# Attention heads as row tiles of TensorE, with both score stages issued together in one fused cross-attention and expert kernel

## The chip, the cores and the metric

The kernel runs on one core of a Trainium2 chip. The metric is the device time of one execution, in microseconds. Inside it five engines work in parallel, each on its own queue in program order and tied to the others by semaphores: PE (TensorE), DVE (VectorE), ACT (ScalarE), POOL (GpSimd) and SP (SyncE, which here only issues DMAs). "PEld" is the loading of PE's stationary operand.

## What is computed

32 sequences of 128 tokens and 128 channels (`x`) attend to 32 contexts of 77 tokens and 96 channels (`ctx`), with 16 heads of 8 channels. A mixture of 8 experts with two chosen per token follows. Cut to what matters:

```
x1  = x + tanh(g_xattn) * attention(layernorm(x), ctx)
        q, k, v = LN(layernorm(x)) @ Wq + bq, LN(ctx) @ Wk + bk, LN(ctx) @ Wv + bv
        w = softmax(q @ k.T / sqrt(8)), one head at a time;  y = w @ v
out = x1 + tanh(g_ffn) * experts(layernorm(x1))
        logits = z @ w_router;  two best experts, softmax over their two logits
        y_e = square(relu(z @ w1[e])) @ w2[e];  out = sum of the two y_e by their gates
```

## The kernel before

The 32 sequences are 8 tiles of 4 batches. One *step* `i` has four *slots* `j` (`slots`, L253), and in a slot each engine works on several batches at once, in an order written out by hand in its `step` function. `near[k]` is the batch `k` places ahead of batch `(i, j)`, so in slot `(i, j)` the first score stage of `near[3]` and `near[2]`, the second of `near[1]` and `near[0]`, the values of `near[-1]` and the routing of `near[-2]` are made, beside two experts (`e[1]`, `e[2]`) of an earlier tile. Steps run from -2 to 9: two steps fill the pipeline, steps 8 and 9 drain it (`closing`, L616). A tile therefore passes every fourth slot.

The attention of a batch has two score stages. The first (`scores`, L496) gives `q @ k.T` with the tokens on partitions, so that DVE can take each head's maximum (`maximum`, L1032, the TENSOR_REDUCE of L1038). Its negative is split into two parts, turned by PE (`max_turn`, L506), copied out by ACT (`max_store`, L745) and written by SP's DMA into rows of the queries' tile (`max_rows`, L341). The second stage (`scoresT`, L513) computes the scores again with the keys on partitions and with those rows added, so that ACT's `exponent` (L815) gives `exp(score - max)` directly. PE multiplies that by the values (`values`, L528), ACT takes the heads out (`evacuate_heads`, L803), PE turns them (`turn_heads`, L552), and DVE scales, adds and takes the statistics (`attended`, L1052: reciprocal, scale, add, stats, aggregate). POOL makes the root (`rstd`, L1381), DVE normalises (`normalise2`, L1082), PE turns the result (`turn`, L559) and routes it (`route`, L564), and DVE picks the two best (`routed`, L1095).

Queries and keys are float32 split into a high and a low part, and the product is taken as three terms (high by high, high by low, low by high), stacked along the contraction: 8 channels of 4 heads by 3 terms is 96 rows. `ks` holds the keys block by block with zeros between heads, so one matmul of 96 rows and 312 columns gives a group of 4 heads in the first stage (4 matmuls a batch), and the second stage takes 16 matmuls of 104 rows and 128 columns a batch. Per tile SP fills these tiles by 8 DMAs of `k_hi` (L324) and 3 of the queries (L338), and POOL by 4 of `k_lo` (L1416).

An expert unit is `hidden` (L577, three matmuls of 512 columns), DVE's `gated` (L1151, relu times the gate, line L1157), ACT's `square` (L821, line L824) and PE's `output` (L589, line L592, eight matmuls). `finish` (L1179) adds a tile's result.

The small PSUM tenants share two banks `ab_0` and `ab_1` in the fixed turn of `AB_USES` (L33). Each use takes the other bank, so a use waits in `claim` (L417) until the use two places before it has been taken out. `keep_on` (L455) issues matmuls without a use for their result.

## Time and profile before

| | us |
|---|---|
| median of 3 runs | 323.77 |
| lowest and highest of them | 321.93, 325.83 |
| the profiled execution, its own time | 321.95 |
| its span (first to last instruction) | 320.2 |
| PE, DVE, ACT, POOL busy in the span | 293.1, 232.8, 178.8, 104.9 |

The profile is of one execution. Busy times are unions over an engine's instructions: PE counts as busy from a matmul's start to its modelled end, so neighbouring matmuls overlap in it. An instruction's "mean ns of one" is its whole length; the distance between the starts of two neighbours is shorter where they are pipelined. The granted clock (PEclk) is a share of 2.4 GHz. A chain piece "DVE u L1157 0.57" is the part of that instruction that lies on the chain of waits.

### The profile page before, as it was taken

Reading aid. Unit: us, or ns where it says so; the run is one execution under the profiler, and the core shown is the slowest. Engines: PE = TensorE matmul, PEld = TensorE weight load, DVE = VectorE, ACT = ScalarE, POOL = GpSimd, SP = SyncE. Lnnn points to the kernel's source line nnn. Section 1 sums busy time; section 2 is a strip of 40 time slices with the busy share of each in tenths; the row PEclk is TensorE's granted clock in tenths of the full one; section 3 lists DMA queues with packets and bytes.
Section 4 is the critical chain, followed back from the end, with each engine's and each line's share of the span. In section 5 each row is a group of like instructions: output and inputs, shape, how many; then the busy total and the mean of one; then the engine's idle time right before and its main releaser. Section 6 shows DMA issues by size and latency. Waiting matters only on the chain.

```text
span 320.2 us, 7854 instructions
## 1 busy us (share of the span) xinstructions
PE 293.1 (92%) x2837; PEld 242.5 (76%) x2837; DVE 232.8 (73%) x934; ACT 178.8 (56%) x412; POOL 104.9 (33%) x193
## 2 busy tenths in 40 slices
PE   7986988799999999998999899999999889989995
PEld 5555576587788788887888787888888778778784
DVE  7886487666869886887688768886767666645765
ACT  1522656544666566654765566566656545565473
POOL 6594415254204712471246224422412210220010
PEclk9997879967999999999999999999999999999998
DMA  3353201087255927593639463917382530070011
GB/s 71 95 152 87 53 12 53 8 138 101 81 191 110 133 75 232 94 126 98 231 67 132 101 196 97 137 26 210 122 130 39 192 125 22 4 269 29 2 35 33
DMA packets 18919, 32.92 MB, mean 103 GB/s; under 512 B 4922, under 2 KB 12059, under 8 KB 18881
## 3 DMA queue, kind: packets, MB, share of 16 engines
q1 hardware_dynamic: 12176, 23.39, 31.1%
q0 software_dynamic: 3216, 7.66, 11.0%
q10 hardware_dynamic: 3488, 1.38, 1.7%
q8 instruction: 22, 0.36, 0.5%
q14 instruction: 17, 0.13, 0.2%
HBM read 21.04 MB, written 2.21 MB: 73 GB/s over the span
## 4 chain that ended last, share of the span: by engine, by line
PE 43%; DMA 21%; DVE 12%; SPq 11%; issue 5%; ACT 4%; ACTq 2%; POOL 1%; DVEq 0%; POOLq 0%
DMA qs<-q_lo 14%; SPq L324 9%; PE y L592 8%; PE c L547 6%; PE ab L503 5%; PE s L524 4%; DMA gb<-gates_scratch 4%; DVE negm L1038 2%; DVE u L1157 2%; PE h L458 2%; SPq L338 2%; PE h L585 2%; PE ab L570 2%; PE h L587 2%; DMA gates_scratch<-gatesT 2%
## 5 line engine op out<-in xcount | busy, mean ns | idle before, releaser
L1038 DVE TENSOR_REDUCE negm<-ab 128x4 f32<-128x308 f32 x128 | 60.6, 476 | 41.4 <-PE ab L503 40.1
L819 ACT ACTIVATE p<-s 77x512 f32<-77x512 f32 x128 | 74.5, 583 | 18.6 <-PE s L524 18.4
L524 PEld LDWEIGHTS s<-qs,ks 104*77 104x77 f32 x512 | 56.8, 155 | 12.6 <-issue 4.6
L524 PE MATMUL s<-qs,ks 104*77 104x128 f32 x512 | 62.2, 246 | 0.8 <-ACT p L819 0.8
L592 PE MATMUL y<-w2s,hs 128*128 128x128 f32 x448 | 60.4, 279 | 1.4 <-ACT hs L824 1.2
L503 PE MATMUL ab<-ks,qs 96*128 96x312 f32 x128 | 50.9, 399 | 8.6 <-DMA qs<-q_lo 4.2
L592 PEld LDWEIGHTS y<-w2s,hs 128*128 128x128 f32 x448 | 55.1, 193 | 3.4 <-ACT hs L824 2.5
L1385 POOL TENSOR_SCALAR rs<-mv 128x1 f32<-128x1 f32 x32 | 7.3, 228 | 144.7 <-DVE mv L1079 144.7
L824 ACT ACTIVATE hs<-u 128x512 f32<-128x512 f32 x56 | 34.9, 623 | 14.5 <-DVE u L1157 14.4
L1157 DVE SCALAR_TENSOR_TENSOR u<-h,gb 128x512 f32<-128x512 f32 x56 | 38.0, 678 | 4.0 <-DMA gb<-gates_scratch 2.5
L503 PEld LDWEIGHTS ab<-ks,qs 96*128 96x128 f32 x128 | 25.3, 198 | 13.5 <-issue 6.2
L547 PE MATMUL c<-p,vs 77*32 77x128 f32 x1024 | 35.4, 280 | 0.0
L585 PE MATMUL h<-x_hi,w_lo 128*128 128x512 f32 x64 | 31.3, 490 | 0.4 <-DVE top L1101 0.4
L805 ACT ACTIVATE oT<-c 128x256 f32<-128x256 f32 x32 | 12.3, 384 | 34.7 <-PE c L547 34.7
L547 PEld LDWEIGHTS c<-p,vs 77*32 77x32 f32 x1024 | 26.6, 111 | 5.1 <-issue 4.8
L587 PE MATMUL h<-x_hi,w_hi 128*128 128x512 f32 x64 | 25.2, 394 | 0.0
L586 PE MATMUL h<-x_lo,w_hi 128*128 128x512 f32 x64 | 25.2, 394 | 0.0
L1416 POOL DMA_DIRECT2D ks<-k_lo x32 | 18.3, 577 | 17.9 <-issue 10.8
L749 ACT ACTIVATE mT<-ab 32x128 fp32r<-32x128 f32 x32 | 8.4, 264 | 24.2 <-PE ab L509 24.1
L1387 POOL TENSOR_TENSOR rs<-rs,neg_half 128x1 f32<-128x1 f32 x32 | 18.3, 572 | 2.7
L1378 POOL TENSOR_TENSOR nrm<-nrm,neg_half 77x4 f32<-77x4 f32 (+1 forms) x16 | 17.3, 1082 | 1.3
L1085 DVE TENSOR_SCALAR xn<-x,mv,rs 128x128 f32<-128x128 f32 x32 | 11.4, 355 | 7.3 <-POOL rs L1387 6.8
(129 smaller groups left out, 503.4 us busy)
## 6 DMA issues: line engine op xcount, KB each, us to landing
gb<-gates_scratch SPq DMA_DIRECT2D x14, 768.0 KB, 5.8
gb<-gates_scratch SPq DMA_DIRECT2D x7, 512.0 KB, 3.9
qs<-q_hi SPq DMA_DIRECT2D x12, 256.0 KB, 6.5
ks<-k_hi SPq DMA_DIRECT2D x60, 39.0 KB
x_res<-in_x_dram POOLq DMA_DIRECT2D x8, 256.0 KB, 5.2
out_dram<-y_out POOLq DMA_DIRECT2D x7, 256.0 KB, 6.3
x_sb<-in_x_dram POOLq DMA_DIRECT2D x6, 256.0 KB, 5.0
qs<-q_lo SPq DMA_DIRECT2D x6, 256.0 KB, 8.7
```

The source lines that it names most:

```text
L324: sp.dma_start(ks[r:r + HD, par, :, i, :].bitcast(F32), k_hi[QROWS * i:QROWS * i + QROWS].rearrange("p b n -> p (b n)").bitcast(F32))\
L503: nc.tensor.matmul(p[:, 0:J * NP].rearrange("t (i n) -> t i n", n=NP), qs[0:QR, par, c, T * j:T * j + T], ks[0:QR, par, c, :, NP * j:NP * ...
L524: mm = nc.tensor.matmul(p[0:N, T * i:T * i + T], ks[:, par, c, i, NP * j:NP * j + N], qs[:, par, c, T * j:T * j + T], start=True, stop=True)
L547: mm = nc.tensor.matmul(bank_c[VT * i:VT * i + VT, r:r + T], vs[:, par, j, NC * i + c, :], p32[:, m % LR, T * i:T * i + T], start=(c == 0) ...
L585: nc.tensor.matmul(p[:, :], w1_lo[:, e, :], x_hi[:, par, :], start=True, stop=False)
L586: nc.tensor.matmul(p[:, :], w1_hi[:, e, :], x_lo[:, par, :], start=False, stop=False)
L587: nc.tensor.matmul(p[:, :], w1_hi[:, e, :], x_hi[:, par, :], start=False, stop=True).then_inc(h_ready, 1)
L592: mm = nc.tensor.matmul(bank_y[:, D * b:D * b + D], hs[:, e % 2, T * b:T * b + T], w2s[:, e, :], start=(e == 0 and b == 0), stop=(e == E - ...
L819: nc.scalar.activation(p32[:, m % LR, :], src, ACT.Exp).then_inc(p_done, 1)
L824: nc.scalar.activation(hs[:, e % 2, :], u[:, e % 2, :], ACT.Square).then_inc(hs_done, 1)
L1038: nc.vector.tensor_reduce(negm[:, :, c], bank_ab[bank][:, 0:J * NP].rearrange("t (i n) -> t i n", n=NP)[:, :, 0:N], AX.X, ALU.max, negate= ...
L1157: nc.vector.scalar_tensor_tensor(out=u[:, e % 2, :], in0=bank_h[e % 2][:, :], scalar=0.0, in1=gb[:, par, e, :], op0=ALU.max, op1=ALU.mult) ...
```

## The change

The heads become row tiles. A head group `i` owns rows `32i` to `32i+31` of `qs` and `ks`: 24 rows of three terms and 2 rows of the maximum. The zeros between heads go. Each head is one matmul of 24 rows and 78 columns in the first stage and one of 26 rows and 128 columns in the second. `both_scores` issues four of them in turn on four different row groups: two of the first stage for one batch, two of the second for another; a call has 16 matmuls and a slot has two calls. The first call (heads of groups `c`, `d` and the second pair of exponents) stands after `turn_heads`; the second (`a`, `b` and the first pair) ends the slot. The values of a batch come first in a slot (behind `turn`) and wait for all its exponents. Keys are projected one slot earlier (slot 2). The three query DMAs of 256 KB become 12 of 64 KB, 4 on SP and 8 on POOL; a maximum takes two DMAs instead of one. The first tile's queries are put in place by matmuls with a selector; tile 1 takes the DMA path. `p32` has 6 buffers instead of 5. The orders of ACT and DVE are rewritten, and the 104-row memsets of `ks` go. In the diff, cut to its core, the lines that the new orders replace are left out; they stand in the kernel above.

```diff
+    (-1, "turn2"), (0, "s1c2"), (0, "s1d2"), (-1, "route2"), (0, "mT2"), (0, "s1a3"), (0, "s1b3"),
+    (-1, "turn3"), (-1, "route3"), (0, "s1c3"), (0, "s1d3"), (0, "mT3"), (1, "v"), (1, "s1a0"), (1, "s1b0"),
+    (0, "turn0"), (1, "s1c0"), (1, "s1d0"), (0, "route0"), (2, "ctxT"), (1, "mT0"), (2, "k"), (2, "xT"),
+    (1, "s1a1"), (1, "s1b1"),
+    (0, "turn1"), (1, "s1c1"), (1, "s1d1"), (0, "route1"), (2, "q"), (1, "mT1"), (1, "s1a2"), (1, "s1b2"),
 ]
...
+        qs = sb("qs", [J * ROWS, 2, NC, GT], F32R)
+        ks = sb("ks", [J * ROWS, 2, NC, G * NP], F32R)
...
+        def stack_keys(eng, s, par, term, i, landing):
+
+            r = ROWS * i + HD * term
+            src = k_lo if term == 1 else k_hi
+            eng.dma_start(ks[r:r + HD, par].rearrange("p c n -> p (c n)").bitcast(F32),
+                          src[ROWS * i:ROWS * i + ROWS].rearrange("p b n -> p (b n)").bitcast(F32))\
+                .then_inc(landing[par], 16)
+
+        def stack_queries(eng, s, par, term, i, landing):
+
+            r = ROWS * i + HD * term
+            src = q_lo if term == 2 else q_hi
+            eng.dma_start(qs[r:r + HD, par].rearrange("p c t -> p (c t)").bitcast(F32),
+                          src[ROWS * i:ROWS * i + ROWS].bitcast(F32)).then_inc(landing[par], 16)
...
+            def stack_q(s, par, term):
+
+                sp.wait_ge(hi_q, s + 1)
+                for i in range(J):
+                    stack_queries(sp, s, par, term, i, q_stacked)
 
             def max_rows(s, par, j):
                 bank, n = ab(s, f"mT{j}")
                 sp.wait_ge(ab_taken[bank], n)
-                sp.dma_start(qs[QR:MR, par, :, T * j:T * j + T].bitcast(F32),
-                             mT[:, j % 2, :].bitcast(F32)).then_inc(m_in[j], 16)
+                for a in range(SPLITS):
+                    sp.dma_start(qs[KEYED + a::ROWS, par, :, T * j:T * j + T].bitcast(F32),
+                                 mT[H * a:H * a + H, j % 2, :].bitcast(F32)).then_inc(m_in[j], 16)
 
             def spread_gates(s, par):
...
+            def both_scores(first, first_pair, second, second_pair):
+
+
+                if first:
+                    s, par, j = first
+                    if j == 0 and first_pair == 0:
+                        stacked(s, par)
+                    banks = [claim(s, f"s1{'abcd'[i]}{j}") for i in (2 * first_pair, 2 * first_pair + 1)]
+                if second:
+                    t, tp, b = second
+                    if t < 2 and (b, second_pair) == (0, 0):
+                        pe.wait_ge(ones_in[tp], 16 * SPLITS)
+                    if second_pair == 0:
+                        pe.wait_ge(m_in[b], SPLITS * (16 * t + 16))
+                    m = NC * (G * t + b) + 2 * second_pair
+                    if m > 0:
+                        pe.wait_ge(p_done, m)
+                for c in range(NC):
+                    if first and (s, j, first_pair) == (0, 0, 0):
+                        pe.wait_ge((q_kept_act, q_kept_dve)[c % 2], c // 2 + 1)
+                    for k in range(2):
+                        if first:
+                            r, (p, ready) = ROWS * (2 * first_pair + k), banks[k]
+                            mm = nc.tensor.matmul(p[:, NP * c:NP * c + NP], qs[r:r + KEYED, par, c, T * j:T * j + T],
+                                                  ks[r:r + KEYED, par, c, NP * j:NP * j + NP], start=True, stop=True)
+                            if c == NC - 1:
+                                mm.then_inc(ready, 1)
+                        if second:
+                            r = ROWS * FIRST_EXPS[2 * second_pair + k]
+                            mm = nc.tensor.matmul(bank_s2[k][0:N, T * c:T * c + T],
+                                                  ks[r:r + SHIFTED, tp, c, NP * b:NP * b + N],
+                                                  qs[r:r + SHIFTED, tp, c, T * b:T * b + T], start=True, stop=True)
+                            if c == NC - 1:
+                                mm.then_inc(s2_ready, 1)
...
+                    pe.wait_ge(p_done, NC * n + NC)
                 r = T * (c // 2)
                 for i in range(J):
                     mm = nc.tensor.matmul(bank_c[VT * i:VT * i + VT, r:r + T], vs[:, par, j, NC * i + c, :],
-                                          p32[:, m % LR, T * i:T * i + T], start=(c == 0), stop=(c % 2 == 1),
+                                          p32[:, (NC * n + FIRST_EXPS.index(i)) % LR, T * c:T * c + T], start=(c == 0), stop=(c % 2 == 1),
                                           skip_group_check=True)
                 mm.then_inc(pv_done, 1)
...
             def turn(s, par, j):
                 pe.wait_ge(post_d, at(POST, G * s + j, "normed"))
-                p, ready = claim(s, f"turn{j}", j in (0, 3) and not last(s))
+                p, ready = claim(s, f"turn{j}")
                 nc.tensor.transpose(p[:, 0:T], xn2[:, :], ident[:, :]).then_inc(ready, 1)
 
             def route(s, par, j):
                 if (s, j) == (0, 0):
                     pe.wait_ge(experts_in, 16 * 3)
-                if last(s):
-                    pe.wait_ge(xT_done, G * s + j + 1)
+                pe.wait_ge(xT_done, G * s + j + 1)
...
                     if near[-1] and not values_first:
                         for c in range(NC):
                             values(*near[-1], c)
+                    if held:
+                        output(*held)
+                    if j == 1 and near[-2]:
                         route(*near[-2])
+                    warm(i, j, 0)
                     if near[-1]:
                         turn_heads(*near[-1])
+                    both_scores(near[2], 1, near[0], 1)
+                    if (i, j) == (0, 0):
+                        project_keys(1)
                     if e[1] is not None:
                         hidden(sf, pf, e[1])
+                    if j != 1 and near[-2]:
+                        route(*near[-2])
+                    if turned and i != -1:
                         transpose_ctx(turned[0])
                     if turned and turned[0] == 0:
                         keep_on(bank_s2[1], 1)
                         project_keys(0)
+                        transpose_x(0)
                     if (i, j) == (-2, 3):
+                        first_queries()
                         keep_on(bank_s2[1], 2)
+                        select_queries()
+                    elif made:
+                        project_queries(made[0])
                     if e[2] is not None:
                         hidden(sf, pf, e[2])
+                    warm(i, j, 1)
+                    if near[2]:
+                        max_turn(*near[2])
+                    if keyed and j == 2:
+                        project_keys(keyed[0])
+                        transpose_x(keyed[0])
+                    if turned and i == -1:
+                        transpose_ctx(turned[0])
+                    if j == 1 and spread(i - 1):
                         gates_turn(i - 1)
+                    if j == 1 and nxt:
+                        project_values(nxt[0])
+                    if e[1] is not None and (i, j) != (S - 1, 2):
                         output(sf, pf, e[1])
+                    warm(i, j, 2)
+                    both_scores(near[3], 0, near[1], 0)
+                    if turned and i == -1:
                         transpose_x(turned[0])
...
                     if j == 1 and exists(i - 1):
                         gate_exp(i - 1)
+                    if near[0]:
                         exponent(*near[0], 2)
+                        exponent(*near[0], 3)
+                    if (i, j) == (0, 0):
+                        evacuate_k(*keyed)
+                    if turned and i != -1:
                         evacuate_ctxT(turned[0])
                     if turned and turned[0] == 0:
                         evacuate_k(*turned)
+                        evacuate_xT(0)
+                    if (i, j) == (-2, 3):
+                        first_queries()
+                        keep_queries()
+                    elif made:
+                        evacuate_q(*made)
+                    if e[1] is not None:
                         squared(sf, e[1])
+                    if near[2]:
+                        max_store(*near[2])
+                    if keyed and j == 2:
+                        evacuate_k(*keyed)
+                        evacuate_xT(keyed[0])
+                    if turned and i == -1:
+                        evacuate_ctxT(turned[0])
+                    if j == 1 and nxt:
+                        evacuate_v(*nxt)
                     if (i, j) in PREPARING:
                         prepare_experts(PREPARING.index((i, j)))
                     if e[2] is not None:
                         squared(sf, e[2])
+                    if near[1]:
+                        exponent(*near[1], 0)
+                        exponent(*near[1], 1)
+                    if turned and i == -1:
                         evacuate_xT(turned[0])
+                    if j == 1 and spread(i - 1):
+                        gate_rows(i - 1)
                     if near[-1]:
                         evacuate_turned(*near[-1])
...
+                    take(ahead, 2)
+                    if near[-2]:
+                        low_x(*near[-2])
+                    if j == 1 and near[-2]:
                         routed(*near[-2])
+                    take(gating)
+                    take(post, 4)
                     take(top_scores)
                     take(post)
+                    take(gating)
+                    take(top_scores, 3)
+                    take(gating, 2)
+                    if i == 0:
+                        take(ahead, 2)
+                    if (i, j) == (0, 0):
+                        take(prepare, 2)
+                    if j == 2 and exists(i - 2):
+                        finish(i - 2, par)
+                    if j != 1 and near[-2]:
+                        routed(*near[-2])
+                    if e[1] is not None:
                         gated(sf, pf, e[1])
+                    take(gating, 3)
+                    if near[-1]:
                         normalise2(*near[-1])
+                    if e[2] is not None:
+                        gated(sf, pf, e[2])
                     take(prepare, 9)
+                    if near[3]:
+                        take(tops_of(near[3]), 2)
...
+            def stack_rest_q(s, par):
+                pool.wait_ge(hi_q, s + 1)
+                apart(pool)
+                for i in range(J):
+                    stack_queries(pool, s, par, 1, i, q_rest_stacked)
+                bank, n = ab(s, "q")
+                pool.wait_ge(ab_taken[bank], n)
+                apart(pool)
+                for i in range(J):
+                    stack_queries(pool, s, par, 2, i, q_rest_stacked)
```

## Rows read from the trace of the kernel before

**Rows 1.** The page, part 1: busy time of PE

```profile
PE 293.1 (92%) x2837; PEld 242.5 (76%) x2837; DVE 232.8 (73%) x934; ACT 178.8 (56%) x412; POOL 104.9 (33%) x193
```

**Rows 2.** The page, part 4: chain that ended last, by engine

```profile
PE 43%; DMA 21%; DVE 12%; SPq 11%; issue 5%; ACT 4%; ACTq 2%; POOL 1%; DVEq 0%; POOLq 0%
```

**Rows 3.** Stretches: length, engines' busy us, granted clock, DMA share, GB/s

```profile
70.00:80.00 10.00, 9.76 (x80) 7.84 (x78) 5.83 (x33) 5.46 (x16) 5.35 (x8) 0.70 0.81 108
...
127.60:161.20 33.60, 31.53 (x343) 27.17 (x342) 26.48 (x112) 20.50 (x50) 12.24 (x22) 1.00 0.62 131
...
290.00:320.00 30.00, 25.17 (x198) 21.44 (x196) 19.02 (x73) 15.98 (x31) 2.43 (x5) 0.97 0.06 19
```

**Rows 4.** Chain of waits, 127 to 166 us: start, us on the chain, what

```profile
128.84 0.68 SPq L324
...
135.84 9.67 DMA qs<-q_lo
...
151.38 0.28 DVE o L1061
...
152.09 0.29 DVE st L1075
...
153.06 0.57 DVE u L1157
153.64 0.40 DVE negm L1038
154.03 0.14 issue
154.17 0.63 PE ab L436 x4
154.80 0.89 PE y L592 x8
155.69 0.11 PE ab L562
...
156.84 1.01 PE c L547 x32
157.85 0.32 PE ab L570 x2
158.17 0.25 PE ab L503
158.42 0.27 PE s L524 x4
158.69 0.24 PE c L556 x2
158.93 0.53 PE ab L445 x2
159.46 0.23 PE h L585
...
161.22 0.86 PE ab L453 x2
```

**Rows 5.** Groups by line and shape: busy us, mean ns | idle before

```profile
L1038 DVE TENSOR_REDUCE negm<-ab 128x4 f32<-128x308 f32 x128 | 60.6, 476 | 41.4 <-PE ab L503 40.1
...
L1157 DVE SCALAR_TENSOR_TENSOR u<-h,gb 128x512 f32<-128x512 f32 x56 | 38.0, 678 | 4.0 <-DMA gb<-gates_scratch 2.5 <-PE h L587 1.6
L824 ACT ACTIVATE hs<-u 128x512 f32<-128x512 f32 x56 | 34.9, 623 | 14.5 <-DVE u L1157 14.4
...
L1416 POOL DMA_DIRECT2D ks<-k_lo x32 | 18.3, 577 | 17.9 <-issue 10.8 <-PE s L524 7.1
...
L805 ACT ACTIVATE oT<-c 128x256 f32<-128x256 f32 x32 | 12.3, 384 | 34.7 <-PE c L547 34.7
...
L1057 DVE RECIPROCAL rden<-c 128x16 f32<-128x16 f32 x32 | 8.1, 252 | 0.8 <-PE c L556 0.8
...
L1183 DVE TENSOR_TENSOR y_out<-x,y 128x512 f32<-128x512 f32 x7 | 4.7, 678 | 2.1 <-PE y L592 2.1
```

443 lines of the change are left out of this document (121 added, 322 removed).

## The prediction

> **What bounds the kernel now.** I read the page's busy times first [rows 1]: PE is busy 293.1 of 320.2 us, and no other engine passes 73%. The chain of waits by engine [rows 2] gives PE only 43%, with 21% on DMA and 11% on SP's queue, so PE is full for most of the time but something beside it ends last now and then. The stretches [rows 3] say how the middle looks: one tile, 127.6 to 161.2 us, takes 33.6 us with PE busy for 31.5 and DVE for 26.5. The chain in order of time [rows 4] then shows the other thing: SP issues eight key DMAs, 0.68 us each, from 128.84, then the queries', and the last of them (135.84) takes 9.67 us to land. It lands at 145.5, and PE's next first-stage matmul waits for it by 1.5 us. So a tile is about 31.5 us of PE work and 1.5 to 2 us of waits: PE bounds it, because the hand-written order lets DVE and ACT run under it.
>
> **The change, part by part.** *The score matmuls.* Before, a batch costs 4 first-stage matmuls 0.25 us apart and 16 second-stage ones, 0.27 us for four [rows 4]: 1.0 + 1.1 = 2.1 us, 8.3 a tile. After, it has two calls of 16. No row shows row groups side by side. The nearest is the values' group, 32 matmuls of 32 output columns on four column groups in 1.01 us, 32 ns each [rows 4], where a full-width one of the output takes 0.89/8 = 111 ns. From below I take half of that, 0.25 us a call (row groups overlap fully, and half the work of each); from above 16 times the 0.27/4 = 67 ns of today's second stage, 1.1 us, if nothing overlaps. I take the 32 ns of the nearest row, 0.5 us, plus 0.15 for getting in and out: 0.65 a call, 5.2 a tile. PE's own work then falls by 3.1 us a tile to about 28.4 (bounds 25.4 to 32). All else equal, that would be the gain.
>
> The row shows 32 ns a matmul with no gap beside the group of values longer than the 0.15 us of its neighbours. The Trainium skill (TensorEngine Tiling (Array Packing), Tiling Modes) says that a change of tiling mode, not of tile, drains the TensorE. Here each slot gains four such changes; the rule gives no time for one, and with an estimated 0.1 us more for each than I have taken a tile would come out 1.6 us longer.
>
> *The order.* All else is not equal, and I take this to decide. In the new order each slot is one ring of steps in which every engine waits for the one before. Walk through a slot of a middle tile, j = 0, with time 0 at the start of PE's `turn`:
> - PE: turn 0.11, values 1.01, output of the held expert 0.89, heads turned 0.24 [rows 4]: 2.35. With the last one's tail and the hand-over, 2.5.
> - DVE can only now begin `attended`, and all that follows stands behind it in its queue: reciprocal 0.25, scale 0.28, add 0.28, each with 0.04 of hand-over, and stats, whose tail the next instruction covers, 0.2: 1.15 together [rows 4, 5]. Then the reductions of c and d, 0.40 from start to start [rows 4], an aggregate between them (0.1), the end of the last reduction (0.1), the two parts of the maximum (an estimate of 0.4 for two short dependent instructions) and the router's two (0.2): 5.25. Only then `gated(e[1])`, 0.66: 5.9.
> - ACT squares it, 0.62 [rows 5], with two hand-overs: 6.6. PE has been through with its first call, both `hidden` and the maximum's transpose at about 5.2, and waits 1.4 us for this.
> - PE: output(e1) 0.89: 7.5. Only then the second call, which makes heads a and b of the next batch: 0.65, 8.15.
> - DVE reduces a (0.48 and 0.04), 0.14 to PE (the "issue" in [rows 4]): 8.8. `turn`, which opens the next slot, claims the bank of a, since each use takes the bank of the use two places before, and all of PE's queue stands behind it.
>
> So this slot is 8.8 us. The other slots of a tile add to the ring:
> - j = 1: five steps of `gate` (difference and four searches, denominator, conversion, comparisons: an estimate of 1.25) stand ahead of gated(e1), and `gates_turn` and `project_values` ahead of output(e1). Gates are ready 0.6 after gated(e1) at 7.15, with a hand-over 7.9; the values' eight matmuls are of the kind that takes 0.89 in rows 4: 8.8; output 9.7, call 10.35, reduction 11.0.
> - j = 2: `finish` 0.68 [rows 5] ahead of gated(e1), so the square ends at 7.25; ACT then stores the maximum (0.27), whose bank `transpose_x` (0.63 in [rows 4]) needs, and output(e1) is behind that: it starts at 8.0 instead of 6.6, slot 10.2.
> - j = 3: the query projection, 0.86 against the keys' 0.53 [rows 4], comes ahead of hidden(e2), and ACT's copy of it (0.69, an estimate from the 0.62 of the square) ahead of the square: 0.5, slot 9.3.
>
> Sum 8.8 + 11.0 + 10.2 + 9.3 = 39.3 us for a tile that takes 33.4 now (33.6 in rows 3; its neighbours 33.4 and 33.0): +5.9, four such tiles (steps 2 to 5): +24. Step 6 has no keys and queries to make: 8.8 + 11.0 + 9.5 + 8.8 = 38.1 against about 33.3: +5. Step 7: slots 0 and 1 as far as they exist: +4. Step 1 has experts only in its second half, and its first half is freed of one output in the ring: +2.4. Steps -2 to 0 have no expert and no such ring. They lose the memsets and the row-wise query projections, gain the selection, and tile 1 now waits for 24 DMAs that SP and POOL issue at 0.6 to 0.7 us each: I take 0, with 4 us to either side. The drain (steps 8, 9) is not touched. Sum 24 + 5 + 4 + 2.4 = +35.
>
> *The transfers.* Before, q_lo could go only after SP's eight key DMAs, and landed 15.5 us after it was made. Now POOL issues it after four DMAs of keys and four of q_hi, 12 times 0.58 us [rows 5] = 7 us in all, and SP issues 8 + 4 at 0.68 = 8.2 us after the maximum's two. In slots of 9 us both have more than 18 us from the projection to the need. Hidden; if slots were 7 us, as PE's work alone would allow, 24 DMAs in 14 us would be as late as now. The second DMA of each maximum, 0.68 us on SP, has a slot to land in. POOL's queue puts `rstd` of the next slot 0 behind q_lo's DMAs: by my walk they are all issued some 3.5 us into that slot, and the statistics come at 4.3. Hidden by 0.8; without that cover up to 2 us a tile.
>
> The profiled execution is 321.95 us (span 320.2 and 1.75 around it); the median shown is 323.77, the lowest 321.93. 321.95 + 35 = 357.
>
> **Rivals.** *A: PE stays the bound and the saving is real.* The ring would have to be shorter than PE's 28.4 us a tile, which asks for slots of 7.1 us where I count 8.8 to 11. For it: DVE is busy only 26.5 us a tile, so it could keep up. Against it: about 5 us of the ring (3.9 of DVE, 0.6 of ACT and the hand-overs) are DVE and ACT alone, between PE steps that need them. It gives 5 us less in each of five tiles, near 297. Chance 0.08.
>
> *B: the ring is there but shorter by a third of what it adds*, since in-order queues overlap more than my hand-overs allow, and the pipeline's filling is quicker by 4 us: 335 down to 322, about no change at the end. Chance of ending within 1%: 0.06; this case up to 340 otherwise belongs to the forecast's own spread.
>
> *C: the granted clock falls.* With the ring PE works 28.4 of 39.3 us, 72%, in place of 93%. For it: at 70 to 80 us, with PE's busy mark at 98% but no experts' matmuls, the clock was 0.70 [rows 3]. Against it: the drain, 290 to 320 us, full of such waits, kept 0.97. If the middle ran at 0.85, the 3.8 us of PE steps in each ring (0.11, 1.01, 0.89, 0.24, 0.89, 0.65) would grow by 0.67, times 26 slots +17: 374. Chance 0.12.
>
> *D: POOL or the small transfers end last*: rstd 2 us late a tile, or the keys' and queries' landing: +2 a tile, 367. Chance 0.10.
>
> *The forecast*, slower by the ring, 357 (own range 342 to 370): 0.64.
>
> **How the numbers follow.** Slower by over 1%: 0.64 + 0.12 + 0.10 = 0.86; same 0.06; faster 0.08. (1% is about what a measurement of this kernel can tell from no change.) The range goes from 320, since A and part of B are below it (0.1), to 380 (0.08 above): it holds both ends of the call's cost, 0.25 to 1.1 us, of which one call a slot lies on the ring: 26 slots times -0.4 to +0.45, -10 to +12 us.
>
> **What would show it.** Right: PE's busy share falls to about 80%, with idle time ahead of L592's output released by ACT's square, and ahead of `turn` released by DVE's reduction, in each slot; values' groups 9, 11, 10 and 9 us apart; no wait of PE for a DMA of queries in the middle; score calls of about 0.5 us. Wrong: values' groups 7 to 8 us apart and PE busy above 90% (A); a clock below 1.00 between 100 and 260 us (C); `normalise2` waiting for POOL in slot 0, or PE for keys or queries (D); calls of 1 us or more, which would put 357 near 370.

## The result, and the profile after

| | before | after |
|---|---|---|
| median of the runs (lowest to highest), us | 322.85 (320.03 to 325.83) | 419.01 (414.55 to 426.7) |
| the profiled execution, us | 321.95 | 414.55 |
| its span, us | 320.2 | 412.8 |
| granted clock over the span | 0.965 | 0.826 |

The changed kernel is slower by a ratio of 1.297, interval 1.279 to 1.315. Some executions of each of these kernels run 1.5% and more above its fastest; the medians count them, the ratios leave them out. The prediction was 357, with a range of 320 to 380: the direction is right and the size is far off, 96 us longer by the medians and 92.6 by the profiled executions, where 35 were forecast.

The page of after, part 1, the clock's row of part 2, and the first line of part 4 (beside [rows 1, 2]):

```profile
PE 335.7 (81%) x3223; PEld 256.7 (62%) x3223; DVE 235.8 (57%) x929; ACT 176.3 (43%) x407; POOL 127.5 (31%) x239
...
PEclk9896865887599579976999759995899669858999
...
PE 55%; DVE 25%; issue 7%; ACT 5%; DMA 4%; SPq 2%; POOL 1%; DVEq 0%; POOLq 0%; ACTq 0%
```

DVE's and ACT's busy times are those of before, within 3 us. PE's rose by 43 us although its score stages take less work: the clock's row shows why, with digits of 5 to 8 in 22 of the 40 slices. Part 4 names DVE for 25% of the chain (12% in [rows 2]) and DMA for 4% (21%).

A good ruler for a kernel of slots is the start of the values' group of each slot, read from PE's timeline. I name them by the slot in which PE issues them; a step is the distance of its four. All sums below are made in the profiled executions.

| stretch, us | before | after | difference |
|---|---|---|---|
| start of the span to the first values, in (0,1) | 39.4 | 43.9 | +4.5 |
| from there to the values of slot (2,0) | 59.6 | 82.9 | +23.2 |
| steps 2 to 6 | 165.9 | 221.3 | +55.5 |
| step 7 | 27.6 | 37.0 | +9.4 |
| the drain | 27.7 | 27.7 | 0 |

Where a slot runs at full clock, the ring can be read off. This is the chain of waits of after, slot (3,0), with its columns start, us on the chain, what:

```profile
170.58 0.30 PE ab L575
170.88 1.01 PE c L560 x32
171.89 1.09 PE y L604 x8
172.98 0.23 PE c L569 x2
173.23 0.27 DVE rden L1051
173.52 0.30 DVE o L1055
173.85 0.30 DVE x L1064
174.17 0.29 DVE st L1069
...
175.90 0.61 DVE u L1151
176.53 0.64 ACT hs L813
177.22 1.16 PE y L604 x8
178.38 0.22 PE ab L526 x2
...
178.98 0.49 DVE negm L1032
179.47 0.14 issue
179.60 0.30 PE ab L575
```

From `turn` at 170.58 to `turn` at 179.60 is 9.0 us, one piece after the other. The second call lies from 178.38 to 178.98, 0.60 us.

The chain counts from end to end and hides what a change of tiling mode costs. The weight loads show it (start, us, engine, line; in brackets the idle time before):

```profile
171.82 0.86 PEld L604 LDWEIGHTS y<-w2s,hs 128*128 128x128 f32 x7 [0.20 <-issue]
...
172.70 0.25 PEld L569 LDWEIGHTS c<-ident,oT 128*128 128x128 f32 x2
173.12 0.18 PEld L526 LDWEIGHTS ab<-ks,qs 24*128 24x128 f32 x1 [0.17 <-issue]
```

Within the output, and on to the turned heads, a weight load starts mostly 1 to 3 ns behind the start of the matmul before it. At each change of mode it starts 0.20 us behind (from the values to the output, from the turned heads to the first call, from the output to the second call, from the first call to `hidden`; 0.200 to 0.208 in nearly all of those at full clock). The Trainium skill (TensorEngine Tiling (Array Packing), Tiling Modes) says that such a change drains the TensorE, and the trace agrees. So the eight matmuls of the held output take 1.09 us on this chain, where the chain of before has 0.89 [rows 4].

Step 2, then slot (3,0) and what comes behind it, in windows (columns as in [rows 3]):

```profile
126.85:171.10 44.25, 37.50 (x401) 28.77 (x405) 28.07 (x114) 20.86 (x51) 16.63 (x31) 0.85 0.46 100
170.90:176.00 5.10, 4.77 (x67) 3.67 (x67) 3.71 (x21) 1.95 (x6) 3.80 (x8) 1.00 1.03 102
176.00:178.00 2.00, 1.04 (x9) 0.79 (x8) 2.00 (x7) 1.40 (x3) 1.23 (x3) 1.00 0.87 87
178.00:179.90 1.90, 1.24 (x25) 0.90 (x24) 1.44 (x8) 0.91 (x3) 0.96 (x2) 1.00 0.51 53
179.90:182.00 2.10, 2.10 (x34) 1.72 (x34) 1.09 (x5) 0.69 (x4) 1.84 (x3) 0.52 0.55 119
182.00:184.00 2.00, 2.00 (x11) 2.00 (x12) 0.00 (x0) 0.21 (x1) 0.00 (x0) 0.50 0.88 139
```

PE waits in the ring (1.04 of 2.00 us busy, then 1.24 of 1.90), and then the granted clock falls from 1.00 to 0.52 and 0.50, that is from 2.4 to 1.2 GHz, while PE is full. The values' group took 1.88 us there instead of 1.01. By the mean granted clock (0.826 of 412.8 us, 0.965 of 320.2) after spends 144 us of its span at the low level, before 22.

In the start the chain shows something else:

```profile
43.96 0.69 SPq L314
...
51.05 0.65 SPq L322
...
51.75 7.72 DMA qs<-q_hi
...
59.66 0.39 PE ab L526 x2
```

SP issues eight key and four query DMAs of tile 1, one each 0.7 us, and the last takes 7.72 us to land. PE waits for it, as the groups say (columns as in [rows 5]):

```profile
L604 PE MATMUL y<-w2s,hs 128*128 128x128 f32 x448 | 74.9, 320 | 10.5 <-ACT hs L813 10.5
...
L526 PE MATMUL ab<-ks,qs 24*128 24x78 f32 x512 | 47.6, 313 | 11.5 <-DMA qs<-q_hi 9.4
...
L575 PE MATMUL ab<-ident,xn 128*128 128x128 f32 x32 | 10.7, 334 | 18.1 <-DVE negm L1032 18.1
```

`turn` waited 18.1 us in total for DVE's reductions and the output 10.5 us for ACT's square: the two waits that the prediction named.

### The profile page after: what moved, and what is told of

Read it like the earlier page. It is cut to its first block, busy times and chain, and to the rows that moved or that the text cites. A ratio compares the mean times of both kernels' runs of the same rounds, so it can differ in the third digit from the quotient of the medians.

```text
span 412.8 us, 8881 instructions
## 1 busy us (share of the span) xinstructions
PE 335.7 (81%) x3223; PEld 256.7 (62%) x3223; DVE 235.8 (57%) x929; ACT 176.3 (43%) x407; POOL 127.5 (31%) x239
## 4 chain that ended last, share of the span: by engine, by line
PE 55%; DVE 25%; issue 7%; ACT 5%; DMA 4%; SPq 2%; POOL 1%; DVEq 0%; POOLq 0%; ACTq 0%
PE y L604 16%; PE c L560 9%; DVE negm L1032 7%; PE ab L526 6%; PE y L457 4%; ACT hs L813 2%; PE ab L575 2%; PE ab L452 2%; DVE u L1151 2%; PE ab L492 2%; DVE x L1064 2%; DVE o L1055 2%; DMA qs<-q_hi 2%; DVE st L1069 2%; PE c L569 2%
## 5 line engine op out<-in xcount | busy, mean ns | idle before, releaser
L1032 DVE TENSOR_REDUCE negm<-ab 128x4 f32<-128x308 f32 x128 | 56.7, 466 | 67.0 <-PE ab L526 67.0
L604 PE MATMUL y<-w2s,hs 128*128 128x128 f32 x448 | 74.9, 320 | 10.5 <-ACT hs L813 10.5
L604 PEld LDWEIGHTS y<-w2s,hs 128*128 128x128 f32 x448 | 65.8, 225 | 22.9 <-ACT hs L813 16.9
L526 PE MATMUL ab<-ks,qs 24*128 24x78 f32 x512 | 47.6, 313 | 11.5 <-DMA qs<-q_hi 9.4
L526 PEld LDWEIGHTS ab<-ks,qs 24*128 24x128 f32 x512 | 40.2, 217 | 26.7 <-issue 22.9
L813 ACT ACTIVATE hs<-u 128x512 f32<-128x512 f32 x56 | 35.1, 626 | 39.0 <-DVE u L1151 38.2
L532 PE MATMUL s<-qs,ks 26*77 26x128 f32 x512 | 36.6, 268 | 0.0
L1051 DVE RECIPROCAL rden<-c 128x16 f32<-128x16 f32 x32 | 8.1, 254 | 36.7 <-PE c L569 36.7
L457 PE MATMUL y<-ident 128*128 128x256 f32 x84 | 29.0, 467 | 0.0
L532 PEld LDWEIGHTS s<-qs,ks 26*77 26x77 f32 x512 | 26.8, 168 | 1.1 <-issue 1.1
L575 PE MATMUL ab<-ident,xn 128*128 128x128 f32 x32 | 10.7, 334 | 18.1 <-DVE negm L1032 18.1
L582 PEld LDWEIGHTS ab<-wr,xT 128*128 128x128 f32 x64 | 12.3, 228 | 15.1 <-issue 14.1
```

Source lines behind the costliest of these rows:

```text
L457: nc.tensor.matmul(bank[:, 0:2 * T].rearrange("p (o t) -> p o t", o=2), ident[:, :], ident[:, :].rearrange("p (o t) -> p o t", o=1).broadc ...
L526: mm = nc.tensor.matmul(p[:, NP * c:NP * c + NP], qs[r:r + KEYED, par, c, T * j:T * j + T], ks[r:r + KEYED, par, c, NP * j:NP * j + NP], s ...
L532: mm = nc.tensor.matmul(bank_s2[k][0:N, T * c:T * c + T], ks[r:r + SHIFTED, tp, c, NP * b:NP * b + N], qs[r:r + SHIFTED, tp, c, T * b:T * ...
L604: mm = nc.tensor.matmul(bank_y[:, D * b:D * b + D], hs[:, e % 2, T * b:T * b + T], w2s[:, e, :], start=(e == 0 and b == 0), stop=(e == E - ...
L813: nc.scalar.activation(hs[:, e % 2, :], u[:, e % 2, :], ACT.Square).then_inc(hs_done, 1)
L1032: nc.vector.tensor_reduce(negm[:, i, :], bank_ab[bank][:, 0:NC * NP].rearrange("t (c n) -> t c n", n=NP)[:, :, 0:N], AX.X, ALU.max, negate ...
```

## The experiments

All kernels but e6 start from the changed kernel. Each block of runs had its own runs of before beside it, with medians of 321.0 to 323.1 us.

**e1, filling matmuls in the ring's waits.** It asks what the clock costs.

```diff
                     if near[2]:
                         max_turn(*near[2])
+                    if near[0] and near[2] and e[1] is not None:
+                        pe.wait_ge(p_done, NC * (G * near[0][0] + near[0][2]) + NC)
+                        keep_on(bank_s2[1], (2, 3, 2, 1)[j])
```

> The kernel after, with 2, 3, 2 and 1 matmuls of no use (256 columns, into the second exponents' bank once it is read) in slots 0 to 3, behind the maximum's transpose, where PE waits for the square. They lie in idle time of 1.4 us and more, so the ring of waits is not made shorter. Theory (two causes: a ring at full clock, and a granted clock at half for 146 us of the 413): the clock stays at 1.00 in the middle, slot 1 falls from some 15 to some 11 us, a tile from 44 to about 40, and the time to 375 to 390. Rival (the ring alone makes the time, the clock is only its mark): within 5 us of 415, or slower by the matmuls added.

Measured: 404.5 us (403.53 to 410.36), ratio 1.254 (1.237 to 1.271); 73 us at the low level instead of 144; step 2 40.8 us instead of 44.0. The expectation of 375 to 390 failed. Halving the time at 1.2 GHz gave back 14.5 us by the medians. In the profiled executions it gave 10.1, a seventh of the 71 us that came back to full clock, and 7.8 of these in steps 2 to 6. Much of a slot is DVE's and ACT's, and something else became late. In step 3 slot 2 took 12.1 us where it takes 10.3 in step 2, and its chain shows why:

```profile
187.29 3.18 DMA gates_scratch<-gatesT
...
190.49 3.79 DMA gb<-gates_scratch
...
194.31 0.70 DVE u L1154
```

The gates go through memory and back. In the new order ACT copies them (`gate_rows`) as the last but one thing of slot 1, behind the exponents, so they come late for the first expert of the next tile. In e1 DVE waits 6.8 us for them in three slots, in after 0.2 us in all: there the slow slots hide it.

**e2, the second call ahead of output(e1); e3, gated(e1) ahead of the reductions.** Two single cuts of the ring.

```diff
@@ e2: PE; in ACT max_store ahead of squared @@
-                    if e[1] is not None and (i, j) != (S - 1, 2):
-                        output(sf, pf, e[1])
                     warm(i, j, 2)
                     both_scores(near[3], 0, near[1], 0)
+                    if e[1] is not None and (i, j) != (S - 1, 2):
+                        output(sf, pf, e[1])
@@ e3: DVE @@
                     take(gating)
+                    if j == 2 and exists(i - 2):
+                        finish(i - 2, par)
+                    if e[1] is not None:
+                        gated(sf, pf, e[1])
                     take(top_scores, 3)
```

> The kernel after, with the slot's second score call put ahead of output(e1) on PE and the maximum's copy ahead of the square on ACT; nothing else moves. Theory of the ring: the ring no longer holds gated(e1), the square and output(e1) (0.66 + 0.62 + 0.1 + 0.9), but the maximum's transpose and copy instead (0.3 + 0.3 + 0.1), so a slot at full clock falls by about 1.4 us from 9.0 and 9.7 to 7.6 to 8.3, PE waits less and the clock falls less often: 350 to 370. Rival (the score calls or the row tiles themselves are dear, the order is not): no more than 10 us are won.

> The kernel after, with DVE's gated(e1) (and finish) put ahead of the second reduction and the maximum's parts; PE's and ACT's orders stay. Theory of the ring: output(e1) is ready 0.6 to 0.7 us earlier in each slot (gated no longer behind 1.05 us of reduction, parts and router), some 26 slots: 15 to 20 us less, more if the clock falls less. Rival: the maximum's transpose becomes late instead and nothing is won (within 5 us of 415).

Measured: e2 422.18 us (ratio 1.299, 1.282 to 1.315), e3 421.11 us (1.300, 1.280 to 1.321). Neither moved the time. Slot 0 at full clock fell from 9.0 to 8.6 us in both. In e3 slot 3 went from 9.6 to 10.2, and slot 2 of steps 2 to 5, partly at half clock, from between 10.3 and 13.3 to between 13.9 and 15.5. The profiled execution of e2 took 439.31 us, 17 above its median, so the lengths of its slots at half clock (up to 15.1) say little; what its chain names stands. In e2's chain the ring closed again through DVE's tail: the reductions of a and b stand behind the second gated, the low part of the queries and the statistics:

```profile
188.12 0.60 DVE u L1151
188.71 0.79 DVE x_st L954 x4
...
189.64 0.38 DVE x_mv L960 x4
190.01 0.37 DVE negm L1032
```

So the ring isn't held by the one dependence that I had taken out. One cut passes it on to the next instruction in DVE's order. (That is read from the chain; no run takes this next one out alone.)

**e4, the order of the row groups in a call.** Is it worth anything that four groups take turns?

```diff
-                for c in range(NC):
+                for stage, k, c in [(stage, k, c) for stage in (0, 1) for k in range(2) for c in range(NC)]:
```

> The kernel after, with the 16 matmuls of a score call in another order: four of one row group, then four of the next, where the kernel after goes to another row group with each. Theory (the groups work side by side, the call takes 0.4 to 0.57 us because of that): a call takes 0.9 to 1.1 us, of which one a slot is on the ring: 10 to 15 us slower. Rival (a call is bound by issuing 16 pairs at some 30 ns, whatever the rows): the call and the time stay the same.

Measured: 421.52 us (418.26 to 422.71), ratio 1.306 (1.291 to 1.321); slots as in after. The mean of a first-stage matmul is 314 ns, of a second-stage one 268, against 313 and 268. At full clock a call takes 0.65 us here and 0.64 in after. That doesn't mean that four matmuls of one group run one behind the other at no cost. The timeline of e4's PE in a call (start, us, engine, line) shows another thing:

```profile
170.23 0.31 PE L526 MATMUL ab<-ks,qs 24*128 24x78 f32 x2
170.25 0.29 PE L532 MATMUL s<-qs,ks 26*77 26x128 f32 x2
170.36 0.29 PE L526 MATMUL ab<-ks,qs 24*128 24x78 f32 x2
170.38 0.31 PE L532 MATMUL s<-qs,ks 26*77 26x128 f32 x4
```

The kernel issues the four first-stage matmuls of one group, then those of the next, then the second stage. But in the trace two of each stage start within 0.04 us, and the next round follows 0.11 us later; the two that end their first-stage groups, known by the semaphores that they raise, are both in the last round. So each round has one matmul of every group. In after the four of a round start within 0.01 us. The groups run side by side in either order, and a call is about as long as one group's own four matmuls, some 0.11 us apart in the first stage.

**e5, filling, the gates' copy ahead, tile 1's transfers ahead.** e1 with one matmul more in slots 0 and 1, and:

```diff
@@ ACT @@
                     if near[2]:
                         max_store(*near[2])
+                    if j == 1 and spread(i - 1):
+                        gate_rows(i - 1)
@@ SP @@
                 for j, near, nxt, third, turned, keyed, made, ffn in slots(i, par):
+                    if (i, j) == (0, 0):
+                        stack_k(*made)
+                        stack_q(*made, 0)
                     if near[2]:
                         max_rows(*near[2])
```

> The kernel after with three things: one more filling matmul in slots 0 and 1 than in the run with the filling alone; the gates' rows copied by ACT before the values and the second square instead of at the slot's end; and for tile 1 SP's key and query DMAs ahead of the maximum's. Theory: what is then left in the middle is the ring alone, with no wait for the gates' broadcast and no half clock, so every tile of steps 2 to 6 takes 40.5 to 41.5 us as the undisturbed ones do (9.0 + 11.9 + 10.3 + 9.6), and PE's wait for tile 1's queries falls from 9.4 to about 5: 388 to 396. Rival (the two marks were not causes): tiles of 43 to 44 us on average, above 400.

Measured: 396.22 us (395.49 to 399.48), ratio 1.245 (1.218 to 1.272). Its two windows, the start and 165 us of the middle:

```profile
43.00:125.20 82.20, 62.16 (x629) 44.95 (x628) 43.76 (x179) 34.55 (x80) 30.96 (x57) 0.76 0.37 73
125.20:290.00 164.80, 141.89 (x1645) 110.99 (x1648) 111.28 (x445) 83.09 (x198) 64.73 (x116) 1.00 0.48 105
```

With the clock at 1.00 and, in these steps, no gates' transfer on the chain, steps 2 to 5 are 41.1, 41.1, 41.1 and 41.2 us, slots 9.1, 12.1, 10.3 and 9.7. That is the ring, 8 us above before's 33.2, with some 0.2 us of filling in slot 1 (e1 has 11.9 there, with one filling matmul fewer). PE's wait in the start fell from 9.4 to 7.1 us only, where about 5 were expected, and it was for another transfer: SP now issues the maximum's DMAs behind the twelve, and the chain names one of these, 8 KB, landing 7.46 us after its issue.

**e6, before's tiles and transfers in after's orders.** It separates the order from the row tiles.

```diff
@@ before's kernel with after's AB_USES and orders; in PE @@
+                    for c in (2, 3):
+                        if near[2]:
+                            scores(*near[2], c)
+                        if near[0]:
+                            scoresT(*near[0], c)
```

> The kernel before, with its block-by-block keys, 96-row and 104-row matmuls and large DMAs, but the orders of the kernel after on PE, ACT and DVE, and its turn of the two shared banks. Theory (the order costs the time, the row tiles save a little): about as slow as the kernel after, 380 to 415, a tile at full clock 41 to 43 us, since its second call on the ring has 1.0 us of matmuls where row tiles have 0.5; the start is some 15 us shorter since tile 1 waits for fewer DMAs. Rival (the row tiles or the small DMAs cost it): below 345.

Measured: 378.91 us (377.35 to 385.99), ratio 1.186 (1.146 to 1.225). Its stretches against before: to the values of (2,0) 102.8 us (+3.7), steps 2 to 6 210.4 us (+44.5), step 7 36.0 us (+8.4). The time is just under the expected 380 to 415. The order by itself costs 56.6 us of span, with what it does to the clock (52 us at the low level) and to the gates (DVE waits 6.2 us for them). What is left to the row tiles and their transfers is 36 us: 24.0 in the start, 10.9 in steps 2 to 6, 1.0 in step 7. The 10.9 isn't the price of the tiles at full clock: e6's step 5, with 3.4 us at the low level, takes 41.0 us, and the row tiles at full clock take 41.1 (e5). Once the order is a ring, a shorter call gains next to nothing in the middle.

**e7, the ring cut in several places at once** (on top of e5's two moves, without the filling): the second call ahead of `gates_turn`, output(e1) and all projections, which go behind it; `finish` ahead of `attended`; head a's reductions ahead of the second gated.

```diff
+                    warm(i, j, 2)
+                    both_scores(near[3], 0, near[1], 0)
                     if j == 1 and spread(i - 1):
                         gates_turn(i - 1)
                     if e[1] is not None and (i, j) != (S - 1, 2):
                         output(sf, pf, e[1])
...
+                    if made and made[0] > 1:
+                        project_queries(made[0])
```

> Row tiles as in the kernel after, with the ring cut: second score call behind the maximum's transpose and ahead of output(e1), maximum's copy ahead of the square, the reductions of a and b ahead of and behind gated(e2) and ahead of statistics, k_lo and q_lo; the projections and gates_turn behind output(e1); the router's matmul of slot 1 ahead of the held output; tile 1's DMAs earlier. Theory: a slot is 7.1 to 8.4 us, a tile 30 to 34, PE busy above 88% and the clock at 1.00 in the middle: 330 to 355. Rival (something of the row tiles themselves, such as drains, holds a slot at 9 us): 380 or more.

Measured: 408.54 us (402.72 to 424.88), ratio 1.27 (1.218 to 1.322): the expectation failed. Slots 0 and 3 came to 8.5 us, slot 1 grew to 18. The waits of e7 name it (engine, line, releaser: total, times, longest):

```profile
DVE x L1072 <- DMA x_res<-in_x_dram: 17.3, 6, 5.4
```

The queries' projection, now last in its slot, holds up their DMAs in POOL's queue, and behind these stands the load of the residual rows:

```profile
223.67 1.52 POOL qs L323 x3
...
227.96 9.42 DMA x_res<-in_x_dram
```

**e8, residual rows loaded two slots earlier; e9, the same with e1's filling.**

```diff
-                    if j == (2 if i == -1 else 3) and i > -2 and nxt:
+                    if j == (2 if i == -1 else 1) and i > -2 and nxt:
                         load_rows(*nxt)
```

> e7's kernel with one edit: POOL issues the load of the next tile's residual rows (x_res) in slot 1 of a step and not in slot 3, where it stood behind the 12 issues of keys' and queries' rows. In e7's profile DVE's x waited for that transfer 6 times, 17.3 us in total, and at two places PE stood still for 5 us (its clock fell to 0.50 behind them). Theory of the late transfer: these waits go and with them the stretches of half clock behind them; 408.5 - 17 - 3 to 8 = 383 to 389 us. Rival, the order of e7 itself (slot 1's gates and values) is what is slow: the waits for x_res go, others end at the same time, 402 to 409 us.

> e8's kernel with e1's filling matmuls (2, 3, 2, 1 in slots 0 to 3) behind the turn of the maxima. Theory: e7 ran some 120 us at half clock; with the filling they become some 60 us, and as in e1 against after a fifth of that comes off: 10 to 15 us under e8, 370 to 378 us. If e8 already keeps its clock (mean over 0.91), the filling changes it by less than 4 us. Against the kernel before: steps at full clock were 8.5 + 11.6 + 9.1 to 11.6 + 8.5 = 38 to 40 us, before's 33.2, so neither comes to before's time; a time under 340 us would make this sum wrong.

Measured: e8 401.38 us, ratio 1.235 (1.221 to 1.249), e9 390.24 us (381.17 to 392.65); both expectations failed. The wait is gone from the list of waits, but the time fell by 7 us only, not 20 or more. In e9 the chain of step 3 ran through `SPq`, twelve issues, and then:

```profile
181.55 11.02 DMA qs<-q_hi
```

As soon as the slots get shorter, the small transfers themselves are what comes last.

**e10, e11: is it the large loads beside them?** The load of a later tile (115 and 256 KB) moved by one slot, in e5 and in e9.

```diff
-                    if (i, j) in ((-1, 3), (0, 1)):
+                    if (i, j) in ((-1, 3), (0, 2)):
                         load(i + 3, 1 - par)
@@ e11 also @@
-                    if j == 0 and i > 0 and exists(i + 3):
+                    if j == 1 and i > 0 and exists(i + 3):
```

> e5's kernel with one edit: POOL issues the load of tile 3 (115 and 256 KB) in slot (0,2) and not in slot (0,1), where it ran beside the small transfers of tile 1's queries: in e5's profile PE waited 7.1 us for them before the scores of (1,0), at 50.8 to 57.9 us. Theory of contention: alone, the small transfers land in some 4 us and not in 7, the wait falls from 7.1 to 3 to 5 us, slot (0,1) from 15.5 to 11.5 to 13.5, and the whole by 2 to 6 us (less half-clock time included) to 390 to 394 us. Rival, the small transfers are slow by their number of descriptors: the wait stays at 6 to 7.5 us and the time at 394 to 398 us.

> e9's kernel with the loads of tiles 3 on moved by a slot in the same manner ((0,1) to (0,2), (i,0) to (i,1)). In e9's profile PE waited 4 times, 12.1 us in total and 9.0 us at most, for the queries' small transfers (issued at 179.4 to 182.2 us, landed at 192.6 us, with 115 and 256 KB loads issued at 185.4 and 186.3 us). Theory of contention: these waits come to under 4 us in total and slot 1 of step 3 from 14.9 to 11 us; 390 - 8 to 14 = 376 to 382 us. Rival: the small transfers wait for one another; the waits stay over 9 us and the time at 387 to 393 us.

Measured: e10 394.58 us (ratio 1.234, 1.216 to 1.253), e11 384.88 us (1.199, 1.178 to 1.221). In e10 the wait of PE was 7.8 us and not shorter, and in e11 10.3 us in 3 waits, 8.4 at most, instead of 12.1 in 4 (9.0). The wait of e10:

```profile
PE ab L529 <- DMA qs<-mT: 7.8, 1, 7.8
```

In the start the rival stands: the transfer that comes last, again a maximum's of 8 KB behind the twelve, lands 8.04 us after its issue without a load beside it. Whether by the number of transfers ahead of it or by something else these runs don't say. For the middle e11 decides nothing: its time lies between the two expectations, and e9's fastest run is below all of e11's. e10's steps 2 to 6 are the cleanest measure of the ring: four times 41.1 and 39.7, from 125.1 to 329.2 us 204.1.

**e12, e13, e14: is the start held by the clock?** Matmuls without a use for their result, on e5. e12: 30 of them in (0,0). It went wrong: each stands in the trace as two matmuls, so one takes 0.43 us and not 0.21, and the wait for tile 1 is in (0,1), so the start became 10 us longer. e13: 15 in (0,1), at the wait. e14: these, and e5's filling in steps 0 and 1 too, 10 in (1,1).

```diff
                     warm(i, j, 2)
+                    if (i, j) == (0, 1):
+                        keep_on(bank_y, 15)
```

> e5's kernel with one edit: 30 matmuls without a use for their result stand in slot (0,0) ahead of the second call of scores, where PE waited 7.1 us for tile 1's small transfers (50.8 to 57.9 us) with the clock at 0.76 and then at 0.52 up to 72 us. At full clock one takes 0.21 us, 6.4 us together, so they end before the wait does. Theory that the clock is a part of the lost start: the stretch behind the wait (57.9 to 72 us, PE busy 12.6 of 14.1) runs at over 0.9, the values of (0,1) to (0,3) stand under 13.5 and under 12 us apart where they stand 15.5 and 12.9, the start is shorter by 3 to 6 us and the time 390 to 393 us. Rival, the clock falls whether or not this wait is filled: the stretch stays at 0.5 to 0.6, the start is the same or up to 3 us longer, 395 to 400 us.

> e5's kernel with 15 matmuls without a use for their result in slot (0,1) ahead of the second call of scores, where PE waits 7.1 us for tile 1's small transfers. One takes 0.43 us at full clock (e12's record), 6.4 us together. Theory that the clock is a part of the lost start: the stretch from 57.9 to 72 us runs at over 0.9 (0.52 in e5), the values of (0,2) stand under 12 us behind those of (0,1) (12.9), the values of (2,0) come at 121 to 123.5 us (125.25) and the time is 391 to 395 us. Rival, the ring makes these slots long: the clock comes back but the values of (2,0) stay within 1 us of 125.25, or the clock falls some us later at the ring's own waits; 395 to 398 us.

> e13's kernel with e5's filling (3, 4, 2, 1 matmuls behind the exponents) in steps 0 and 1 too, and 10 in slot (1,1), where PE waits for the gates. Theory of the clock: 43 to 125 us run at over 0.9 (0.77 in e5) and the values of (2,0) come 4 to 8 us earlier than 125.25 us; 387 to 392 us. Rival, the ring: the clock rises to over 0.9 but the slots stay at 11.5 us or more, as the filling takes the time that it gives: values of (2,0) at 124 to 128 us, 395 to 399 us.

Measured: e12 402.45 us (ratio 1.255, 1.248 to 1.263), e13 395.1 us (1.234, 1.222 to 1.246), e14 397.59 us (391.47 to 401.99). The values of (2,0) came at 134.9, 125.7 and 128.4 us, where e5 has them at 125.25. Windows of e14:

```profile
57.90:72.00 14.10, 10.97 (x113) 7.86 (x111) 6.77 (x26) 5.99 (x13) 0.80 (x2) 0.88 0.01 3
72.00:90.00 18.00, 15.17 (x144) 10.85 (x145) 11.61 (x49) 7.26 (x19) 10.36 (x20) 0.73 0.38 63
90.00:103.00 13.00, 10.79 (x103) 8.50 (x103) 6.58 (x35) 3.90 (x11) 4.47 (x7) 0.98 0.44 67
```

In e5 the clock was 0.52 in the first of these stretches and 0.71 in the last. Here it is 0.88 and 0.98, and the start is 3 us longer all the same: filling there takes at least the time that the clock gives. In e13 the wait itself was filled (PE idle 2.2 us of 7.1) at clock 1.00, and the clock still fell to 0.52 behind it. So filling doesn't mend the start. It puts no price on the start's clock either, since the filling itself takes time. In e12 the wait for tile 1 was over before PE was through; (0,1) then took 8.8 us, before's 9.0. So that slot's excess is the wait for the transfers. The later ones, some 12 us and more in (0,2), (1,1) and (1,2), stay in all of these. In after's chain none of the three holds a transfer. In (0,2), at half clock behind the wait, the largest piece is the kernel's own `keep_on`, 2.9 us with the first two; in (1,1) the gates' steps and the values' projection (L492, 1.7 us at half clock) stand in the ring as in the middle. How much of each is the clock's and how much the order's is left open.

No version beat the kernel before. The lowest median with row tiles was e11's, the lowest with the new order e6's.

## Why the prediction missed

**Right: the ring.** The walk through slot j = 0 gave 8.8 us and the chain shows 9.0, piece by piece: gated ends 5.9 after `turn` (5.9), the square 6.6 (6.6), the output 7.8 (7.5), the second call 8.4 (8.15). The call was taken at 0.65 and measured 0.60. Small errors cancel: 0.11, 1.01, 0.89 and 0.24 make 2.25 and not the 2.35 of the walk, and the same four take 2.63, since `turn` behind its wait takes 0.30 and the held output, behind the change of tiling mode, 1.09; DVE's part then is 3.3 us and not 3.4. Output(e1) takes 1.16 instead of 0.89: it starts after a wait, and the call behind it changes the mode. The prediction read no gap beside the values and gave 0.1 us more a change as an estimate outside its sum; the trace has 0.20 us from a matmul to the next weight load, on the ring twice a slot. Of the signs named for "right", PE at 81% (about 80 was said), `turn` released by DVE's reduction, the output by ACT's square and no wait for queries in the middle are there. Slots of 9, 11, 10 and 9 us aren't: only slots 0, 2 and 3 come to that, and only where the clock is full. The sign for C, a clock below 1.00 between 100 and 260 us, is there too.

Slot 1 is 11.9 us at full clock (e1), not 11.0. This is its chain, with `turn` at 133.93:

```profile
142.06 0.28 PE h L586
142.34 0.89 PE ab L492 x8
...
143.32 0.84 ACT vs L792 x2
144.16 0.35 issue
144.50 0.27 PE ab L526
```

`gates_turn` (L586) starts 8.1 us behind `turn` (7.9 was said) and takes 0.28, for which the walk had nothing. The values' projection (L492) follows as said. But then the second call doesn't wait for the output, 0.89: it waits for ACT's copies of the projected values, from 143.23 to 144.50, 1.27 us. In e5 and e10 one more filling matmul delays `gates_turn` by 0.4 us, and the slot is 12.1.

Slots 2 and 3 are 10.3 and 9.7 (10.2 and 9.3). In slot 2 the walk's own terms, 7.25, 0.27 and 0.63, make 8.15 and not 8.0, which gives 10.35. A tile's ring is 41.1 us with the filling (e10) where 39.3 was said; in place of +29 for steps 2 to 6 it makes +38, and +6.8 in step 7 in place of +4.

The Trainium skill says that tiling speeds up TensorE but not what empties its results (TensorEngine Tiling (Array Packing), PSUM Bottleneck). The trace agrees as far as the maximum goes: DVE's reductions are busy 56.7 us after 60.6, and PE waits 18.1 us for them.

**Wrong, the largest: "Steps -2 to 0 ... I take 0, with 4 us to either side", and +2.4 for step 1.** The start came out 27.7 us longer. I had counted the 24 issues at 0.6 to 0.7 us, and set them against "more than 18 us from the projection to the need", which is true of a tile in the middle. In the start the need comes in the next slot. From SP's first key DMA at 43.96 to the landing at 59.47 is 15.5 us, 7.7 of issues and 7.7 of landing, and PE stands still for 9.4 of them. This sum, done for (0,1), would have shown most of the slot's excess of 8.8 us. (0,2) adds 4.8, (0,3) 0.9, step 1 8.8, the first values 4.5. The sentence that steps -2 to 0 have "no such ring" failed too: in (0,2) and in (1,1) the chain goes through the same reductions and copies without experts. e6, with the old tiles in the same order, has a start of only +3.7: so 24 of the 27.7 us come with the row tiles and how they are filled. The half clock behind the wait is in these 24, and no run prices it apart.

**Wrong: the clock (rival C at 0.12, priced +17 on top).** It was left out of the forecast because the drain keeps 0.97 [rows 3] with waits as many. But the forecast's own premise, PE at 72 to 80% with gaps of 1 to 1.5 us in every slot, was C's condition, so C was no rival to the forecast but part of it. Its price was about right: after's steps 2 to 6, at a mean clock of 0.84, are 17.3 us longer than e10's, which keeps its clock. e10 also has its gates copied earlier, but that isn't what after lacked: after's chain holds no transfer from 60 to 370 us, and DVE waits for the gates' transfer 0.2 us in all. So the 17.3 are the clock's, less what the filling takes. The gates' copy, which I had not looked at, matters once the clock is back: without moving it, filling won 7.8 of the 17.3 (e1).

**The sum once more.** Ring 38.2 in steps 2 to 6 (29 said) and 6.8 in step 7 (4); clock 17.3 in steps 2 to 6 and 2.6, clock and gates together, in step 7 (0); start 27.7 (2.4): the measured 92.6 us of span. Of the miss of 57 us, 25 is the start, 20 the clock, 12 the ring's size.

Rivals A and B fell: the order alone, with no row tile in it, costs 56.6 us (e6). B's own number doesn't follow from its words: a third less of 35 us and 4 us less in the start make 341, not 322 to 335. D held only in the start in this kernel; it became true of the middle as soon as the ring was shortened (e7 to e9).

## What to carry to other kernels

When PE's work is made smaller in a kernel whose order is written by hand, walk one slot through all engines' queues first: the reordering that came with the tiles cost more than the tiles could have given (3.1 us a tile by the prediction's sum), and no single cut gives it back. Price the filling of the pipeline by itself, since a transfer with 18 us of slack in the middle may have none there. If the forecast says that PE will wait in every slot, the clock's price belongs in the sum and not among the rivals.

## What was not expected of the hardware

- Four row groups run side by side even where the kernel issues four matmuls of one group in a row: they start within 0.04 us, and the call takes 0.65 us (e4), with four in turn 0.64 (after).
- A change of tiling mode shows as 0.20 us from the last matmul's start to the next weight load, where it is 1 to 3 ns between full-width matmuls (after).
- The 64 KB DMAs of queries' rows cost SP 0.65 us to issue, each, and the last of a row of twelve issues landed after 7.7 us (after) and 11.0 us (e9), though they carry a quarter of the bytes of before's. A maximum's DMA of 8 KB behind such a row, with the large load moved away, landed after 8.0 us (e10).
- The clock was at 0.5 behind two waits of PE of 1 us and less, with PE full by then, from 180 to some 193 us of after; with such waits filled it was 1.00 for 165 us (e5). Filled at one long wait only, it still fell right behind it (e13).
